# A hand-written schedule for attention: value products in two bursts per group instead of three, 25 other places moved

## The reference

```python
x = x + attn(layernorm(x), W_attn, b_attn, W_proj, b_proj)   # 16 heads of 16 channels, causal
x = x + moe(layernorm(x), ...)                               # 8 experts, top 2, and a shared expert

# attn
qkv = x @ W_attn + b_attn
q, k, v = split(qkv); q, k = rope(q), rope(k)                # rope by head index
att = softmax(where(causal, q @ k.T / sqrt(hd), -inf))
y = (att @ v) @ W_proj + b_proj
```

## Time and profile before

| | us |
|---|---|
| runs of the kernel before | 2012.45 median of 3 (2010.08 to 2017.69) |
| the profiled execution | 2011.82 |
| its span, first to last instruction | 2009.7 |
| PE busy | 1705.4 |
| DVE busy | 1169.7 |
| ACT busy | 860.8 |
| POOL busy | 773.9 |

### The profile page before, as it was taken

One profiled execution on the slowest core, in us unless ns is written; L12 is line 12 of the kernel. 1 busy time (PEld: TensorE's weight loads), 2 busy tenths in 40 slices (PEclk: granted clock), 3 DMA queues, 4 the chain that ended last, 5 costly groups with the idle time before them and its releaser, 6 DMA issues. The chain is left out here.

```text
span 2009.7 us, 42862 instructions
## 1 busy us (share of the span) xinstructions
PE 1705.4 (85%) x14226; PEld 1035.8 (52%) x14227; DVE 1169.7 (58%) x2091; ACT 860.8 (43%) x1257; POOL 773.9 (39%) x1003
## 2 busy tenths in 40 slices
PE   2689999999999998659941299499999999999997
PEld 2344544545455454347620166265666666666664
DVE  6567888888888887644740177375333333333332
ACT  1366666666666665523310022253333333333332
POOL 1133433333333333330057400603555555555554
PEclk9799999999999999969975599799999999999999
DMA  2322332333333332134530062122333333333332
GB/s 73 96 79 82 99 117 88 104 106 99 99 100 96 96 92 88 39 129 154 158 86 17 23 190 86 33 79 61 59 59 58 58 58 58 58 57 58 58 58 42
DMA packets 168693, 163.16 MB, mean 81 GB/s; under 512 B 29681, under 2 KB 159217, under 8 KB 168562
## 3 DMA queue, kind: packets, MB, share of 16 engines
q1 hardware_dynamic: 138354, 125.66, 20.7%
q0 software_dynamic: 30208, 35.81, 11.5%
HBM read 100.82 MB, written 60.30 MB: 80 GB/s over the span
## 5 line engine op out<-in xcount | busy, mean ns | idle before, releaser
L843 ACT ACTIVATE prob<-pair_t 128x1024 f32<-128x1024 f32 x320 | 327.7, 1024 | 270.2 <-PE pair_t L1615 265.5
L670 POOL TENSOR_SCALAR_AFFINE_SELECT prob<-prob 128x256 f32<-128x256 f32 (+1 forms) x448 | 198.0, 456 | 505.6 <-ACT prob L843 495.9
L1507 PE MATMUL pair_s<-wbuf,xt 128*128 x1632 | 374.4, 379 | 1.0 <-DVE xt L1395 1.0
L779 POOL DMA_INDIRECT out_x<-ysb,tok_rows x136 | 215.4, 1584 | 239.0 <-ACT ysb L968 193.3
L1409 DVE SCALAR_TENSOR_TENSOR hb<-pair_s,h_s,sg 128x512 f32<-128x512 f32 x200 | 149.9, 750 | 267.9 <-PE pair_s L1507 200.3
L1400 DVE TENSOR_TENSOR htl<-pair_t,hth 128x512 f16<-128x512 f32 x200 | 138.1, 690 | 240.1 <-ACT hth L932 223.2
L1507 PEld LDWEIGHTS pair_s<-wbuf,xt 128*128 128x128 f16 x1632 | 159.7, 98 | 163.0 <-issue 1.1
L932 ACT CAST hth<-pair_t 128x512 f16<-128x512 f32 x200 | 116.4, 582 | 243.4 <-PE pair_t L1792 121.8
L925 ACT ACTIVATE sg<-pair_s,silu_s 128x512 f32<-128x512 f32 x200 | 137.4, 687 | 190.6 <-PE pair_s L1507 138.8
L1507 PE MATMUL pair_s<-wsh,xt 128*128 128x512 f16 x768 | 188.7, 396 | 15.3 <-DVE xt L1395 8.4
L968 ACT ACTIVATE ysb<-bank,row_w 128x256 f32<-128x256 f32 x136 | 64.6, 475 | 309.3 <-PE bank L1507 309.3
(11 more groups left out here) (228 smaller groups left out, 2741.1 us busy)
## 6 DMA issues: line engine op xcount, KB each, us to landing
q_op<-qk_d SPq DMA_DIRECT2D x192, 64.0 KB, 2.4
k_op<-qk_d SPq DMA_DIRECT2D x192, 64.0 KB, 2.4
x_in<-in_L_attn_x SPq DMA_DIRECT2D x16, 512.0 KB, 4.1
qk_d<-qkh SPq DMA_DIRECT2D x32, 256.0 KB, 2.2
qk_d<-qkl SPq DMA_DIRECT2D x32, 256.0 KB, 2.4
xres<-in_L_attn_x SPq DMA_DIRECT2D x16, 512.0 KB, 4.5
x_d<-x SPq DMA_DIRECT2D x32, 256.0 KB, 2.1
xhl_d<-xhl SPq DMA_DIRECT2D x32, 256.0 KB, 2.4
```

What stands on the lines that cost most here:

```text
L670: last = nc.gpsimd.affine_select(out=v, in_=v, compare_op=ALU.is_ge, fill=0.0, base=0, pattern=[[0, v.shape[1]], [1, P]], channel_multipli ...
L779: pool.indirect_dma_start(out=out, out_offset=bass.IndirectOffsetOnAxis(ap=tok_rows[:, k, 0:1], axis=0), in_=ysb[:, k % ROWS_AHEAD], in_of ...
L843: nc.scalar.activation(prob[:, half, u].rearrange("p a n -> p (a n)"), pair_t[:].rearrange("p a n -> p (a n)"), ACT.Exp, scale=exp_by).the ...
L1507: last = nc.tensor.matmul(out, a, m, start=(i == 0), stop=(i == n - 1))
```

## The change

Numbers in tables change, and no function does. MIX moves the first piece of the value products from step 0 to step 2 of a group. The other tables move work among the twenty steps; some SP transfers move with them. The diff of the tables, with the lines that the prediction speaks of and most others:

```diff
-        MIX = (0, 2, 2, 3)
-        XN_T, XN_HIGH, XN_LOW = ((0, 1), (0, 2)), ((0, 1), (0, 2)), ((0, 1), (0, 3))
-        QK, QK_HIGH = ((0, 4), (1, 4), (2, 4), (3, 1)), ((1, 0), (2, 0), (3, 0), (3, 4))
-        QK_LOW = ((1, 0), (2, 0), (3, 0), (0, 1))
-        V_PROJ, V_PROJ_B, VALUES = ((1, 2), (2, 1)), ((1, 3), (2, 1)), ((1, 3), (2, 3))
-        QK_STORE, QK_LOAD = ((2, 3), (0, 2)), ((2, 3), (0, 3))
-        STATS, VARIANCE, RSTD, SHIFT = ((1, 0), (1, 2)), (1, 4), (1, 4), (2, 1)
-        NORMALISE = ((2, 2), (2, 3), (2, 3), (3, 3))
-        O_T = ((1, 4), (2, 2), (3, 2), (0, 1))
-        DIVIDE = ((2, 1), (2, 2), (3, 2), (0, 2))
-        Y_T, Y_OUT = ((2, 3), (0, 3)), ((3, 1), (0, 4))
-        PROJ, PROJ_B = ((3, 3), (1, 1)), ((3, 4), (1, 1))
+        MIX = (2, 2, 2, 3)
+        XN_T, XN_HIGH, XN_LOW = ((0, 1), (0, 3)), ((0, 1), (0, 3)), ((0, 2), (0, 4))
+        QK, QK_HIGH = ((1, 0), (1, 4), (3, 0), (3, 3)), ((1, 3), (2, 3), (3, 2), (0, 0))
+        QK_LOW = ((1, 2), (2, 2), (3, 2), (0, 1))
+        V_PROJ, V_PROJ_B, VALUES = ((1, 3), (2, 3)), ((1, 3), (2, 4)), ((1, 3), (2, 4))
+        QK_STORE, QK_LOAD = ((2, 3), (0, 3)), ((2, 3), (0, 4))
+        STATS, VARIANCE, RSTD, SHIFT = ((0, 1), (0, 2)), (0, 4), (0, 4), (2, 1)
+        NORMALISE = ((2, 3), (2, 4), (3, 2), (3, 2))
+        O_T = ((1, 3), (2, 0), (2, 2), (2, 4))
+        DIVIDE = ((1, 4), (2, 0), (2, 3), (3, 1))
+        Y_T, Y_OUT = ((2, 1), (0, 0)), ((2, 1), (1, 0))
+        PROJ, PROJ_B = ((3, 1), (1, 1)), ((3, 4), (1, 1))
...
-        X1, X1_STATS, X1_VARIANCE = ((3, 4), (1, 1)), ((0, 0), (1, 2)), ((0, 4), (2, 4))
-        RSTD_B, ROWS = ((0, 4), (3, 0)), ((1, 3), (3, 1))
-        HIGH, LOW = ((1, 4), (3, 1)), ((2, 0), (3, 3))
-        XRES, ROWS_OUT = (1, 2), ((2, 1), (3, 4))
+        X1, X1_STATS, X1_VARIANCE = ((3, 4), (1, 1)), ((0, 3), (2, 1)), ((1, 0), (2, 4))
+        RSTD_B, ROWS = ((1, 1), (2, 4)), ((1, 2), (3, 1))
+        HIGH, LOW = ((1, 3), (3, 2)), ((1, 3), (3, 3))
+        XRES, ROWS_OUT = (1, 2), ((1, 4), (3, 4))
```

More of the change, by code:

```diff
@@ L259, in build @@
         LAG, MAXIMA, M_ROWS, M_SP, O_OUT = 8, 0, 1, 2, 3
-        MIX = (0, 2, 2, 3)
-        XN_T, XN_HIGH, XN_LOW = ((0, 1), (0, 2)), ((0, 1), (0, 2)), ((0, 1), (0, 3))
-        QK, QK_HIGH = ((0, 4), (1, 4), (2, 4), (3, 1)), ((1, 0), (2, 0), (3, 0), (3, 4))
-        QK_LOW = ((1, 0), (2, 0), (3, 0), (0, 1))
-        V_PROJ, V_PROJ_B, VALUES = ((1, 2), (2, 1)), ((1, 3), (2, 1)), ((1, 3), (2, 3))
-        QK_STORE, QK_LOAD = ((2, 3), (0, 2)), ((2, 3), (0, 3))
-        STATS, VARIANCE, RSTD, SHIFT = ((1, 0), (1, 2)), (1, 4), (1, 4), (2, 1)
-        NORMALISE = ((2, 2), (2, 3), (2, 3), (3, 3))
-        O_T = ((1, 4), (2, 2), (3, 2), (0, 1))
-        DIVIDE = ((2, 1), (2, 2), (3, 2), (0, 2))
-        Y_T, Y_OUT = ((2, 3), (0, 3)), ((3, 1), (0, 4))
-        PROJ, PROJ_B = ((3, 3), (1, 1)), ((3, 4), (1, 1))
-        X_BIAS = ((1, 4), (3, 2), (3, 2), (3, 2))
-        X1, X1_STATS, X1_VARIANCE = ((3, 4), (1, 1)), ((0, 0), (1, 2)), ((0, 4), (2, 4))
-        RSTD_B, ROWS = ((0, 4), (3, 0)), ((1, 3), (3, 1))
-        HIGH, LOW = ((1, 4), (3, 1)), ((2, 0), (3, 3))
-        XRES, ROWS_OUT = (1, 2), ((2, 1), (3, 4))
+        MIX = (2, 2, 2, 3)
[10 more added lines that the diff above has]
+        PROJ, PROJ_B = ((3, 1), (1, 1)), ((3, 4), (1, 1))
+        X_BIAS = ((1, 4), (1, 4), (2, 0), (3, 3))
+        X1, X1_STATS, X1_VARIANCE = ((3, 4), (1, 1)), ((0, 3), (2, 1)), ((1, 0), (2, 4))
+        RSTD_B, ROWS = ((1, 1), (2, 4)), ((1, 2), (3, 1))
+        HIGH, LOW = ((1, 3), (3, 2)), ((1, 3), (3, 3))
+        XRES, ROWS_OUT = (1, 2), ((1, 4), (3, 4))
         PREP_MAX, PREP_TOP, PREP_SCALE, PREP_SUM = (0, 4), (1, 0), (1, 1), (1, 1)
```

## The result

The changed kernel takes 2120.03 us (median of 4, 2118.11 to 2122.2), the kernel before 2011.26 (median of 4). The ratio is 1.054 (95% interval 1.0514 to 1.0563). The forecast was 2126, in 2080 to 2162.

The account below looks back on a forecast made before the run. The loop scores, row maxima, scores was taken as the spine. Steps +100, shift rows -21, `x_in` +4 and clock +34 made +117 on 2011.8, or 2129; the forecast said 2126, range 2080 to 2162.

Parts of the forecast that it names:

- Steps 1.2 and 2.2: DVE waits there for a round trip through PE and ACT: next maxima at 6.4 and 6.67, +3.9 and +4.2 us.
- pricing rule: DVE work between row maxima is free up to 0.6 us; a DVE wait there costs all of itself.
- second effect: V_PROJ in 1.3 and 2.3 waits for `qkl` too, so PE stands 2.5 and 3.0 us.
- list of signs: Expected in the changed trace, among others: `qkl` in 1.2 and 2.2 waiting 3 to 4 us for `qkh`, 30 times.
- The other steps: Per batch: 3.2 +0.5; 1.0, 2.0, 3.0 together -2.85; 0.2 +0.7; 1.1 +1.05; thirteen more -0.85 us.
- the term of +6.65 a batch: Sum of all step changes in an undisturbed batch, giving 53.3 us; fifteen batches pay it, +100.
- The burst: Three value products, 2.0 us on PE in step 2 of each group; +0.7 in 0.2, lighter step 0 worth little.
- Late shift rows: ROWS_OUT of the first half moves to 1.4, its stores ahead of the shift copies: -21 us, bounds 12 and 27.
- `x_in`: STATS moves to 0.1 while the load stays at the top of the batch: 0.3 us a batch, +4.
- The clock: Half clock behind the new PE stands of 2.5 and 3.0 us: 22 times 1.5 us, +34, bounds 0 and 60.
- its +45: Clock loss by the skill's rule, if all 30 PE stands pay, instead of +34; sum 11 us higher.
- The rival "faster": Shift-row and `qkl` gains win if both round trips cost under 4.3 us; 1990 us at 3 us; chance 0.03.

Follow-up runs that it names:

- experiment 1: Changed kernel with the high halves of i = 0 and 1 back ahead of their low halves (QK_HIGH (1,1), (2,1)): 1997.81 us, ratio 0.991.
- experiment 2: Changed kernel with only the high half of i = 0 back ahead of its low half (QK_HIGH (1,1), (2,3)): 2074.8 us, one execution.
- experiment 3: Kernel before with only the two round trips put in (QK_HIGH, QK_LOW, V_PROJ, V_PROJ_B later), value products still in three bursts: 2138.76 us, ratio 1.0618.
- experiment 10: Changed kernel with the low halves moved to the step of their late high halves (QK_LOW (1,3), (2,3)): 2115.02 us, ratio 1.0522.
- experiment 5: Kernel before with only the burst of three value products put in (MIX (2, 2, 2, 3)): 1907.43 us against 1859.95, ratio 1.0268.
- experiment 9: Changed kernel, high halves still late, with three bursts of value products again (MIX (0, 2, 2, 3)): 2169.68 us, ratio 1.0793.
- experiment 4: Kernel before with ROWS_OUT of the first half one step later, (2,2), so shift copies are issued ahead of the stores: 1993.24 us, ratio 0.9892.
- experiment 7: Changed kernel with high halves early as in experiment 1, and the input statistics at their old places: ratio 0.993, attention 746.6 us.

## Why the prediction was right, point by point

The span's +108.2 is +2.9 ahead of batch 0, +18.8 in batch 0 (65.5 against 46.7), +85.8 in batches 1 to 14, +0.9 in batch 15 and -0.3 behind. By the steps of the forecast:

- **Steps 1.2 and 2.2.** Forecast 6.4 and 6.67; measured 6.07 and 6.61. Experiments 1, 2 and 3 show that they carry the loss. The pricing rule behind them, that a DVE wait costs all of itself, was too simple: experiment 10 cut 73 us of that wait and gained 2, since other waits of DVE took its place. The forecast had named TensorE's wait in V_PROJ as a second effect; experiment 10 points to it as the one that sets the end. The wait of `qkl` in 2.2, 4.68, is what the working of that step gives; the "3 to 4" in the list of signs was too low for it.
- **The other steps.** 3.2 came at 2.76 (2.9), 1.0 at 2.08 (2.05), 2.0 at 1.81 (1.96), 0.2 at 2.52 (2.7), 1.1 at 2.75 (2.9), all in batch 8. The hand schedule was a little long nearly everywhere; 3.0 was too short, 2.18 (1.96). Taking off the clock's share below, batch 8 is 54.3 - 2.4 = 51.9 where I had 53.3, so the term of +6.65 a batch was +5.25, 21 us too much over fifteen.
- **The burst.** Sized right where it stands (1.93 us for 24 matmuls), judged wrong. "Step 0 of a group is 1.0 lighter on TensorE, which is worth little" holds in the old table (experiment 5) and not in the new one, where 1.0 and 3.0 carry projections: experiment 9 puts it at 49 us. This did not harm the sum, because the redone steps 1.0, 2.0 and 3.0 had the lighter TensorE in them.
- **Late shift rows.** -21 forecast. The waits fell from 25.2 to 1.8, and fifteen batches before had 26.9 above the undisturbed pace; if all of that is gone, as the waits say, the upper bound was right. The 26.3 of experiment 4 are like it in size but made up otherwise: an undisturbed batch there takes 45.97 in place of 46.65, which is 10, and the late copies are only 16 (its fifteen batches lie 11.2 above their undisturbed pace in place of 26.9).
- **`x_in`.** +4 forecast, 0.3 a batch. Wrong in its place: batch 3 waited 1.1, and batch 0 8.9 us, because its load is issued at 66.00, behind the prologue's transfers on SP, and lands 7.7 us later. A steady batch was all that I had scheduled. The fifteen batches lie 16 above fifteen times batch 8, 11.2 of it in batch 0 and 2.9 in batch 3, so this term was 12 too small. In the timeline of DVE, batch 0, steps 0.1 and 0.2:

```profile
63.62 1.23 DVE L1107 TENSOR_REDUCE mx<-pair_s 128x2 f32<-128x1024 f32 x1 [0.81 <-PE pair_s L1587]
73.73 0.75 DVE L993 BATCH_NORM_STATS2 st<-x_in 128x6 f32<-128x256 f32 x2 [8.89 <-DMA x_in<-in_L_attn_x]
```

- **The clock.** +34 forecast for 22 stretches at 1.5. In batches 2 to 14 there are 26: one is in step 0.4 of batch 3, some 6 us behind the wait for `x_in`, and 25 follow the 26 stands of TensorE. Only the stand of 2.46 in batch 12 had none, so the stands of 2.46 us nearly all paid, where I had let half of them go free. One is worth 1.46 behind step 1.2 (1.3 and 1.4 took 3.62 + 2.19 with it in batch 8 and 2.50 + 1.85 in batch 12, which had none there) and about 0.96 behind 2.2 (2.3 to 3.0: 7.61 here, 6.65 in experiment 1, which has none; this holds as far as the clock is all that differs there): 2.4 a batch, 36 in all. The Trainium skill's rule that a wait repeated each turn is paid each turn (TensorE: Matmul & The Clock Gate, "HAM oscillation — how this bites in real kernels") agrees with the trace in its count, 25 of 26; its +45 came from my price of 1.5 for each.

So the sign and the mechanism were right, and 2126 against 2120 owes something to luck, in errors that cancel: 21 us too much in the steps and 6 too little gain from the shift rows, against 12 too little for batch 0's input and other disturbed batches, 3.5 outside these fifteen batches, 2 of clock, and the 3 that the forecast took off without a row for it.

The rival "faster" has a slip. By the prediction's own terms the sum without the clock is +83, or 5.5 a batch, so the sign turns if the two round trips cost under 8.1 - 5.5 = 2.6 us together, not 4.3, and at 3 us the time would be about 2018, not 1990. The two steps came 7.7 us longer together (6.07 - 2.52 and 6.61 - 2.43), and nothing else hangs on this.

The round trip of i = 1 is worth 25.7 us more than that of i = 0 (experiment 2), 1.7 a batch. The steps behind the two waits show where (means of batches 3 to 13). The waits themselves count the same: mending i = 0 takes 3.56 from step 1.2, and mending i = 1 takes 3.56 from 2.2. But 1.3 and 1.4 together fall by 0.27 only (5.68 to 5.41), since without the stand 1.3 still takes 3.52, with TensorE behind its burst by two V_PROJ and a transpose. Steps 2.3 to 3.0 fall by 1.69 (8.35 in experiment 2, 6.66 in experiment 1). And experiment 2 loses 0.49 there against the changed kernel (7.86): in seven of its eleven batches the half-clock stretch behind 2.2 lasts 6.8 us in place of 3.4, and these batches take 8.5 to 8.8 for 2.3 to 3.0 where the others take 7.9. Why the stretches get longer there stays open.

## What to carry to other kernels

When an order is written as tables for several engines, check every producer and consumer pair for a turn: a consumer in step n whose producer is issued in step n + 1 waits for a whole round trip if the loop's spine goes through both. Look for the resource at the end of such a chain (here one PSUM bank that TensorE wants back) before moving the consumer; moving it only renames the wait. And price a moved piece by what stands in its new step on that engine: the same MIX entry cost 33 us or more in one table (experiment 5) and gained 49 in the other (experiment 9). Redo the first and last turns of the loop as well as a steady one.

## What the runs showed of the hardware that I had not expected

The kernel before took 2010 to 2018 us in three of the lots and 1860 in the fourth, on another chip. Attention is not what differs, as far as two kernels of nearly the same order show: it took 749.7 (experiment 1) on the one and 746.6 (experiment 7) on the other. Behind attention the profiled executions took 1188.5 us and 1036.9. On the slower chip TensorE is busy 38.9 of the 150 us from 1000 to 1150 (experiment 1), and on the other 146.7 of them (experiment 7); what it waits for was not followed up.

The late shift rows of the kernel before have two parts. The copies are issued late: SP stands for LOW, then issues 0.5 MB of stores and the four copies of 1 KB behind them. In batch 6 the last copy is issued at 378.93 and lands 1.7 us later, and the wait of 0.8 is all due to the late issue. In batch 5, at the same spacing to the stores, the last copy takes 3.9 us to land, and the wait is 2.9. Time from issue to landing of the last two copies of batch 5 and of the last one of batch 6, in the kernel before:

```profile
DMA to landing us min/median/max: 1.7/2.8/3.9
...
DMA to landing us min/median/max: 1.7/1.7/1.7
```

Such slow copies are strewn over the run. Of 252 shift copies in attention the median takes 1.75 us, and over 3 us are taken by 14 in the kernel before, 7 in the changed one and 10 in experiment 4. In the kernel before, five of the 14 are in step 2.2, in batches 2, 5, 7, 12 and 14: the five batches with waits of 2.4 us and more. In experiment 4, where the copies stand ahead of the stores, four of the 10 are in step 2.2 still, and TensorE waits 0.7 us at most for them. So the earlier issue is what helps, by giving a slow copy room; what makes a copy slow stays open.
